# Second attention's projections in halves over sixteen units, weight splits in quarters, and GpSimd's adding transfers behind the norm pairs of the third attention

## The reference, cut to what matters

```python
x = x + tanh(g_xattn[1]) * _L1_xattn_ref(_layernorm(x), ctx, wq, wk, wv, wo, ln_w)   # second attention
x = x + tanh(g_ffn[1])   * _L1_ffn_ref(_layernorm(x), base_W, gate_W, lora_A, lora_B)
x = x + tanh(g_xattn[2]) * _L2_xattn_ref(_layernorm(x), ctx, Wq, bq, Wk, bk)         # third attention
x = x + tanh(g_ffn[2])   * _L2_ffn_ref(_layernorm(x), w1, w2, w3)

def _L1_xattn_ref(hidden_states, ctx, wq, wk, wv, wo, ln_w):
    x = rmsnorm(hidden_states, ln_w)
    q = (x @ wq.T)  in 32 heads of 16;  k, v = ctx @ wk.T, ctx @ wv.T  in 8 heads of 16, each for 4 query heads
    attn = softmax(q @ k.T / sqrt(16))                  # 256 tokens x 64 keys, per head and batch
    return concat(attn @ v) @ wo.T

def _L2_ffn_ref(x, w1, w2, w3):                         # w1, w2, w3 first rounded to 4-bit NF4 codes
    return (silu(x @ dq(w1).T) * (x @ dq(w2).T)) @ dq(w3).T
```

## Time and profile before

| | |
|---|---|
| median of 3 executions | 1507.81 us (1503.71 to 1510.55) |
| the profiled execution | 1506.91 us |
| its span, first to last instruction | 1505.2 us |
| TensorE busy | 1345.6 us, 89% of the span |
| VectorE busy | 1123.2 us, 75% |
| ScalarE busy | 677.1 us, 45% |
| GpSimd busy | 339.4 us, 23% |
| mean granted clock of TensorE | 0.952 of 2.4 GHz |

### The profile page before, as it was taken

One profiled execution on the slowest core, in us unless ns is written; L12 is line 12 of the kernel. 1 busy time (PEld: TensorE's weight loads), 2 busy tenths in 40 slices (PEclk: granted clock), 3 DMA queues, 4 the chain that ended last, 5 costly groups with the idle time before them and its releaser, 6 DMA issues.

```text
span 1505.2 us, 18648 instructions
## 1 busy us (share of the span) xinstructions
PE 1345.6 (89%) x6492; PEld 966.2 (64%) x6492; DVE 1123.2 (75%) x2045; ACT 677.1 (45%) x1405; POOL 339.4 (23%) x380
## 2 busy tenths in 40 slices
PE   8999999999998989977999998999999999999105
PEld 5665566566575648736888875777777777777102
DVE  4788898888888996976555576666666566568998
ACT  4778777877433443432222224443434444443104
POOL 1112122212164020233111021312222212213620
PEclk9999999999999999988999998999999999999557
DMA  5678888788810011323211210101101101000001
GB/s 218 170 179 184 226 225 197 173 221 213 224 43 1 1 57 34 79 64 79 71 42 42 96 71 1 71 28 43 71 29 43 69 13 61 1 1 1 0 0 56
DMA packets 37910, 127.74 MB, mean 85 GB/s; under 512 B 4944, under 2 KB 10960, under 8 KB 31680
## 3 DMA queue, kind: packets, MB, share of 16 engines
q1 hardware_dynamic: 26304, 83.38, 16.0%
q0 software_dynamic: 11520, 43.26, 15.1%
HBM read 72.63 MB, written 10.75 MB: 55 GB/s over the span
## 4 chain that ended last, share of the span: by engine, by line
PE 57%; DVE 23%; DVEq 6%; ACT 6%; DMA 4%; issue 2%; POOL 1%; POOLq 1%; SPq 0%
PE PS L150 12%; PE PS L152 11%; PE PS L151 11%; DVE AR L676 5%; PE PS L925 4%; PE PS L963 4%; DMA AR<-AR 3%; ACT s_sb L606 2%; DVE AR L2601 2%; PE PS L949 2%; DVE AR L2590 2%; DVE AR L2597 2%; DVEq L666 2%; DVE AR L682 1%; PE PS L535 1%
## 5 line engine op out<-in xcount | busy, mean ns | idle before, releaser
L438 POOL DMA_DIRECT2D AR<-AR x76 | 75.7, 1127 | 334.4 <-DMA AR<-AR 133.5
L151 PE MATMUL PS<-R16r 128*128 128x512 f32 (+1 forms) x328 | 122.1, 372 | 0.0
L535 PE MATMUL PS<-R,PT 128*128 128x512 f32 x256 | 116.1, 596 | 3.7 <-DVE X L716 3.7
L510 PE MATMUL PS<-R,HT 128*128 128x256 f32 x512 | 116.5, 381 | 3.2 <-ACT R L595 3.1
L152 PE MATMUL PS<-R16r 128*128 128x512 f32 (+1 forms) x312 | 119.1, 382 | 0.0
L510 PEld LDWEIGHTS PS<-R,HT 128*128 128x128 f32 x512 | 94.8, 190 | 16.2 <-ACT R L595 4.6
L1083 ACT COPY AR<-PS 128x512 f32<-128x512 f32 x64 | 37.5, 586 | 146.1 <-PE PS L152 145.7
L606 ACT ACTIVATE s_sb<-PS,sm 128x64 f32<-128x64 f32 x256 | 78.2, 338 | 53.4 <-DVE sm L701 52.8
L150 PE MATMUL PS<-HTr,R16r 128*128 128x512 f32 (+1 forms) x240 | 90.7, 378 | 4.6 <-DVE R16r L190 2.5
L150 PE MATMUL PS<-R16r,HTr 128*128 128x512 f32 (+1 forms) x224 | 90.2, 403 | 0.0
L152 PE MATMUL PS<-HTr,R16r 128*128 128x512 f32 (+1 forms) x240 | 87.7, 365 | 0.0
(11 more groups left out here) (313 smaller groups left out, 3495.0 us busy)
## 6 DMA issues: line engine op xcount, KB each, us to landing
AR<-AR POOLq DMA_DIRECT2D x76, 528.0 KB, 6.7
OR<-in_wo SPq DMA_DIRECT2D x12, 1024.0 KB, 12.4
dequantised<-AR SPq DMA_DIRECT2D x8, 1056.0 KB, 5.5
WR<-in_w0q SPq DMA_DIRECT2D x8, 1024.0 KB, 11.5
AR<-in_w3q SPq DMA_DIRECT2D x8, 1024.0 KB, 4.9
WR<-dequantised SPq DMA_DIRECT2D x22, 256.0 KB, 2.8
AR<-in_nf SPq DMA_DIRECT2D x4, 1056.0 KB, 9.4
nf_in<-in_nf SPq DMA_DIRECT2D x4, 1056.0 KB, 10.6
```

Source lines behind the costliest of these rows:

```text
L151: nc.tensor.matmul(out, ah, bl, start=False, stop=False)
L438: nc.gpsimd.dma_start(nf_below(g)[:, part], what[:, part], accum_op=ALU.add, max_dma_last_dim=4 * N_NF // 2).then_inc(added, 16)
L510: i = nc.tensor.matmul(bank(2 + u % 2)[:, tt * 256:(tt + 1) * 256], HT0[:, c, tok], m[:, :, c * B + b, :], start=c == 0, stop=c == C - 1)
L535: i = nc.tensor.matmul(bank(5 + tt), PT[:, at:at + P], vo[:, pr, b, :], start=pr == 0, stop=pr == 1)
```

## The change

In the second attention the eight output tiles and the queries of batches 2 and 3 are cut into halves (12 matmuls with 256 columns, or 6 with 512), and `projections(u)` deals them over all sixteen units: one half in twelve of the units, two halves in units 3, 6, 8 and 14. The adds on VectorE move with them. GpSimd's two weight splits become four quarters each, where a quarter also waits for a count of `probs`, that is, for a `norm` on VectorE to have ended. ScalarE's two copies for the feed-forward's weights move from units 8 and 9 to 7 and 8. At the third attention's end GpSimd's second adding transfer moves behind the norm pairs, a wait for all normed tiles of norm 4 stands in front of `pool_f2(pool, (1,))`, and two calls of `dve_stats` on VectorE move behind `norm_scaled` and `norm_low` calls.

```diff
@@ -1476,7 +1476,12 @@
             spread_keys(pool, 2)
             spread_keys(pool, 3)
             pool.wait_ge(A1["o_hi"], 1)
-            pool_low(Oh[:], Ol[:], OR[:]).then_inc(A1["o_split"], 1)
+            for c in range(C):
+                cols = slice(c * D, (c + 1) * D)
+                if c:
+                    pool.wait_ge(A1["probs"], c)
+                i = pool_low(Oh[:, cols], Ol[:, cols], OR[:, cols])
+            i.then_inc(A1["o_split"], 1)
 
         def u_kbd(hc, b):
             at = (hc * B + b) * HC1 * SK
@@ -1511,19 +1516,18 @@
             return (ORr[:, 0:HG * S], ORr[:, HG * S:2 * HG * S]) if b % 2 else (OTh, OTl)
 
         def pe_a1(pe):
-            def project_q(b, pr):
-                if b:
+            def project_q(b, pr, halves=(0, 1)):
+                if b and halves[0] == 0:
                     pe.wait_ge(A1["qT_ready"], 2 * b - 1 + pr)
-                if b >= 3 and pr == 1:
-                    pe.wait_ge(A1["acc"], 2 * b - 4)
-                for hh in range(2):
+                for hh in halves:
                     hc = 2 * pr + hh
                     for c in range(C):
                         w = slice(c * D + hc * P, c * D + (hc + 1) * P)
                         tok = slice(b * S, (b + 1) * S)
                         i = mm3(bank(1 - pr)[:, hh * S:(hh + 1) * S], Wh[:, w], Wl[:, w], HTh[:, c, tok],
                                 HTl[:, c, tok], c == 0, c == C - 1)
-                i.then_inc(A1["q_mm"], 1)
+                if halves[-1]:
+                    i.then_inc(A1["q_mm"], 1)
 
             def scores(u):
                 b, hc = divmod(u, C)
@@ -1557,21 +1561,53 @@
                                          PT[:, pr * S:(pr + 1) * S], start=True, stop=True)
                 i.then_inc(A1["pv_mm"], 1)
 
-            def project_o(b, tt):
-                if tt == 0:
-                    pe.wait_ge(A1["olo"], (b + 1) * C)
-                    if b == 0:
-                        pe.wait_ge(A1["o_split"], 1)
+            def project_o(b, tt, halves=(0, 1)):
+                if halves[0] == 0:
+                    if tt == 0:
+                        pe.wait_ge(A1["olo"], (b + 1) * C)
+                        if b == 0:
+                            pe.wait_ge(A1["o_split"], 1)
+                    else:
+                        pe.wait_ge(A1["qT_ready"], 2 * B)
+                    if b:
+                        pe.wait_ge(A1["acc"], 2 * b - 1 + tt)
+                hi, lo = out1(b)
+                for half in halves:
+                    for hc in (2 * half, 2 * half + 1):
+                        tok = slice(hc * S + tt * P, hc * S + tt * P + P)
+                        i = mm3(bank(0 if tt else 7), hi[:, tok], lo[:, tok], Oh[:, hc * D:(hc + 1) * D],
+                                Ol[:, hc * D:(hc + 1) * D], hc == 0, hc == C - 1)
+                if halves[-1]:
+                    i.then_inc(A1["wo_mm"], 1)
+
+            def projections(u):
+                if u < 2:
+                    project_q(2, 0, (u,))
+                elif u == 2:
+                    project_q(2, 1, (0,))
+                elif u == 3:
+                    project_q(2, 1, (1,))
+                    project_q(3, 0, (0,))
+                elif u == 4:
+                    project_q(3, 0, (1,))
+                elif u == 5:
+                    project_q(3, 1, (0,))
+                elif u == 6:
+                    project_q(3, 1, (1,))
+                    project_o(0, 0, (0,))
+                elif u == 7:
+                    project_o(0, 0, (1,))
+                elif u == 8:
+                    project_o(0, 1)
+                elif u < 13:
+                    project_o(1, (u - 9) // 2, ((u - 9) % 2,))
+                elif u == 13:
+                    project_o(2, 0, (0,))
+                elif u == 14:
+                    project_o(2, 0, (1,))
+                    project_o(2, 1, (0,))
                 else:
-                    pe.wait_ge(A1["qT_ready"], min(2 * b + 6, 2 * B))
-                if b:
-                    pe.wait_ge(A1["acc"], 2 * b - 1 + tt)
-                hi, lo = out1(b)
-                for hc in range(C):
-                    tok = slice(hc * S + tt * P, hc * S + tt * P + P)
-                    i = mm3(bank(0 if tt else 7), hi[:, tok], lo[:, tok], Oh[:, hc * D:(hc + 1) * D],
-                            Ol[:, hc * D:(hc + 1) * D], hc == 0, hc == C - 1)
-                i.then_inc(A1["wo_mm"], 1)
+                    project_o(2, 1, (1,))
             pe.wait_ge(A1["w_split"], 1)
             pe.wait_ge(lo_ready, T + 2)
             project_q(0, 0)
@@ -1592,10 +1628,7 @@
             for u in range(NU):
                 b, at = divmod(u, C)
                 turn_p(u)
-                if at < 2 and b:
-                    project_o(b - 1, at)
-                if at > 1 and b + 2 < B:
-                    project_q(b + 2, at - 2)
+                projections(u)
                 if u == NU - 1:
                     pe_norm_tile(pe, 3, 0)
                     pe_norm_tile(pe, 3, 1)
@@ -1668,8 +1701,8 @@
                 nc.scalar.copy(PT[:], bank(4, 2)).then_inc(A1["pt_ready"], 1)
                 if u + 2 < NU:
                     exps(u + 2)
-                if at > 1 and b + 2 < B:
-                    queries(b + 2, at - 2)
+                if u in (1, 3, 5, 7):
+                    queries(2 + u // 4, u // 2 % 2)
                 act.wait_ge(A1["pv_mm"], u + 1)
                 if u == C:
                     act.wait_ge(A1["o_split"], 1)
@@ -1677,11 +1710,11 @@
                 if u == NU - 2:
                     act_a2_keys(act, 0)
                     act_a2_keys(act, 1)
-                if u == 8:
+                if u == 7:
                     act.wait_ge(F1["w_in"], 16)
                     act.wait_ge(A1["q_mm"], 2 * B)
-                    nc.scalar.copy(Wh[:, 0:C * NWF // 2], WR[:, 0:C * NWF // 2])
-                if u == 9:
+                    nc.scalar.copy(Wh[:, 0:C * NWF // 2], WR[:, 0:C * NWF // 2]).then_inc(F1["w_hi"], 1)
+                if u == 8:
                     nc.scalar.copy(Wh[:, C * NWF // 2:C * NWF], WR[:, C * NWF // 2:C * NWF]).then_inc(F1["w_hi"], 1)
 
         def act_a2_keys(act, dc):
@@ -1724,14 +1757,24 @@
                 hi, lo = out1(b)
                 nc.vector.tensor_tensor(lo[:, cols], bank(6)[:, 0:S], hi[:, cols].bitcast(F32), ALU.subtract)\
                     .then_inc(A1["olo"], 1)
-                if 0 < hc < 3 and b:
-                    add(b - 1, hc - 1)
-                    if hc == 2:
-                        dve_stats(dve, b - 1)
+                if u == 8:
+                    add(0, 0)
+                elif u == 9:
+                    add(0, 1)
+                    dve_stats(dve, 0)
+                elif u == 11:
+                    add(1, 0)
+                elif u == 13:
+                    add(1, 1)
+                    dve_stats(dve, 1)
+                elif u == 15:
+                    add(2, 0)
             norm_low(dve, 3, 0)
             norm_scaled(dve, 3, 2)
+            add(2, 1)
             norm_low(dve, 3, 1)
             norm_scaled(dve, 3, 3)
+            dve_stats(dve, 2)
             add(B - 1, 0)
             add(B - 1, 1)
             dve_stats(dve, PAIRS - 1)
@@ -1756,17 +1799,22 @@
             sp.dma_start(OR[0:EH, 0:2 * D], lb_d).then_inc(F1["b_in"], 16)
 
         def pool_f1(pool):
-            pool.wait_ge(F1["w_hi"], 1)
-            pool_low(Wh[:, 0:C * NWF], Wl[:, 0:C * NWF], WR[:, 0:C * NWF]).then_inc(F1["split"], 1)
+            for c in range(C):
+                cols = slice(c * NWF, (c + 1) * NWF)
+                pool.wait_ge(A1["probs"], NU // 2 + c)
+                pool.wait_ge(F1["w_hi"], c // 2 + 1)
+                i = pool_low(Wh[:, cols], Wl[:, cols], WR[:, cols])
+            i.then_inc(F1["split"], 1)
             pool_norm(pool, 3)
             accumulate(pool, LATE, 1)
-            accumulate(pool, LATE, 2)
             pool_norm_pair(pool, 4, 0)
             pool_norm_pair(pool, 4, 1)
             pool_f2(pool, (0,))
             pool_norm_pair(pool, 4, 2)
             pool_norm_pair(pool, 4, 3)
+            accumulate(pool, LATE, 2)
             accumulate(pool, LATE, 3)
+            pool.wait_ge(hn_ready, T * 5)
             pool_f2(pool, (1,))
             pool_norm(pool, 5)
             accumulate(pool, LATE, 4)
@@ -2096,12 +2144,11 @@
             norm_scaled(dve, 5, 0)
             norm_scaled(dve, 5, 1)
             sums((6, 7))
+            norm_scaled(dve, 5, 2)
+            norm_low(dve, 5, 0)
+            norm_scaled(dve, 5, 3)
+            norm_low(dve, 5, 1)
             dve_stats(dve, 2)
-            norm_low(dve, 5, 0)
-            norm_low(dve, 5, 1)
-            norm_scaled(dve, 5, 2)
-            norm_scaled(dve, 5, 3)
-            dve_stats(dve, 3)
 
 
 
@@ -2316,6 +2363,7 @@
             norm_low(dve, 5, 3)
             norm_scaled(dve, 5, 4)
             norm_scaled(dve, 5, 5)
+            dve_stats(dve, 3)
```

## The result

The changed kernel takes 1496.91 us (median of 6 runs, 1495.79 to 1498.74) where the kernel before takes 1508.7 (median of 6 beside it, 1501.99 to 1510.78): a ratio of 0.9934, 95% interval 0.9917 to 0.995. The forecast was 1494.0, range 1488.5 to 1500.5. Its profiled execution has a span of 1494.0 us (1495.79 with what lies around it) for 1505.2 before.

What follows compares the result with a forecast made beforehand. VectorE and TensorE were taken to bound the second attention by turns, a chain through all engines the third attention's end. Gains 7.8 + 3.6 + 1.6 = 13.0 us off 1506.9 gave 1494, range 1488.5 to 1500.5.

Steps and rivals of the forecast that it cites:

- Second attention, 7.8 forecast: Units 0 to 15 and last outputs: halves hidden in TensorE's idle time gain 8.85 us, less 1.05 at the outputs.
- Unit 14, 7.35 forecast: Second attention: two halves make `weigh` late with the key wait behind it, so the unit takes 7.35 us, not 5.5.
- The quarters never meet a multiply: Second attention: each GpSimd quarter, some 1.7 us, ends before VectorE's next multiply; being late costs up to 1.7.
- rival 3: Second attention: TensorE's clock falls once in the loop or quarters meet a multiply; 3 to 4 us, 1497.5, chance 0.16.
- the idle 3.13: Second attention: TensorE's 3.13 us idle while GpSimd's whole split holds VectorE's multiply; rows at 1.2 GHz follow; expected to go.
- Third attention's end, 3.6 forecast: Scalings moved behind both `norm_scaled`: 3.6 us gained of the 6.0 or 4.4 the chain would give.
- The stall: Third attention, second half: GpSimd's scalings now hold VectorE's L360, which ends at 665.5 where it ended at 669.2.
- rival 2: Third attention's end: VectorE gets in between GpSimd's instructions; second part gives 6.0, total 1491.5, chance 0.16.
- rival 4: Third attention's end: second addition lands after 6.7 us, delaying third addition and scalings; 1497.5 to 1500, chance 0.12.
- rival 6: Behind the touched stages: something unseen gives the gain back; 1502 to 1507, chance 0.05.
- Statistics, 1.6 forecast: Before the third feed-forward: one statistics call moves behind the last low part, so TensorE's first product starts 1.6 us sooner.
- Rivals 3 and 5: rival 3 has its line; 5: the clock stays down in the second attention's loop, 3.2 us per unit, chance 0.05.

Runs made afterwards that it cites:

- e4: The changed kernel with both of GpSimd's weight splits whole again instead of in quarters: 1502.2 us, ratio 0.9961.
- e5: The kernel before with only GpSimd's two weight splits of the second attention cut into quarters: 1506.61 us, ratio 0.9992.
- e1: The kernel before with only the second attention's part of the change (halves, moved adds, quarters, earlier copies): 1502.52 us, ratio 0.9971.
- e6: The changed kernel with a GpSimd drain behind the first and second of the second weight tile's three scalings: 1497.24 us, ratio 0.9937.
- e7: The changed kernel with GpSimd's second weight tile's scalings waiting until VectorE is past the second half's L360: 1494.56 us, ratio 0.9909.
- e11: The kernel of e8 measured again, beside the changed kernel on the same chip: 1493.6 us, ratio 0.991.
- e2: The kernel before with only GpSimd's new order at the third attention's end: 1504.75 us, ratio 0.9979.
- e10: The changed kernel unaltered, measured and profiled a second time: 1497.34 us, ratio 0.9938.
- e3: The kernel before with only the two statistics calls moved later on VectorE: 1507.26 us, ratio 0.9996.
- e8: As e7, with the first weight tile's scalings also waiting for the first `norm_scaled` pair: 1493.98 us, ratio 0.9913.

## Why the prediction was right

**Second attention, 7.8 forecast, 7.0 and 6.7 measured** (loop and output step, 102.16 before, 95.13 and 95.46 after). A half is hidden and the unit is VectorE's: yes, 5.51. Unit 14, 7.35 forecast: 7.47. Unit 10, 7.85; units 11 to 13, 17.25 together for 17.15. Off by little everywhere: two halves cost 0.75 and not 0.6, in units 3 and 6, and the step to the last outputs 1.23, not 1.05. The quarters never meet a multiply, and what the whole split cost was seen rightly as L360's 2.35 us: e4 and e5 have 2.4. But the prediction, and its rival 3 with it, tied the rows at 1.2 GHz in the earlier trace rows to the idle 3.13. In e5 that idle time is gone (0.77), and the `scores` are at 1.2 GHz all the same (3.78, as in the kernel before). In the changed kernel, with half a piece ahead of `weigh`, they take 1.99 behind an idle 2.02; in e1, e6, e7 and e11 the clock falls there. What decides it stays open.

**Third attention's end, 3.6 forecast.** The chain did what was worked out, with the clock up: from the pair to L360 6.0 us less (15.63 to 9.61). The stall took the place foreseen: L360 of the second half 3.01 for 0.43, 2.6 back, 3.4 left. The Trainium skill ("SBUF — State Buffer", Who interferes with whom) has the loser of the shared port pair block for the other's instruction. That agrees with the rows of the kernel before shown with e6, where VectorE waits for one instruction of a run (L676 3.03 for 2.36); at the second weight tile's scalings it does not, for there VectorE waited for all three (5.13 for the pair before, L360 3.01, and 3.21 in e2). So rival 2's mechanism is real on this chip, and the trace that the prediction read had it at 640.65, beside the case against it at 653.6; for the scalings that counted it was wrong, and nothing in the prediction says why, so that this term came out right by the nearest row and not by an understood cause. Its 2.4 us were real: e7 gets 2.58 in that column by moving the scalings out of the way. The third addition waited for the second: its two halves were issued 5.5 and 8.5 us after the second's first issue (644.68 to 650.17 and 653.15), and the scalings began 9.0 after it, forecast 8.8. In this two errors cancel. The second addition's later half took 7.4 us to land, not 6.7 at most, which is rival 4's beginning; and the scalings followed the last issue by 0.57, where 1.33 behind the first of two had been put in.

What the forecast had not seen lies between the first feed-forward and that pair, in "end 1": either the first `norm_scaled` pair is held by GpSimd's first scalings (0.75, in the changed kernel's first profile), or TensorE's clock falls behind an idle time of 2 us (1.2 to 1.7), or both (e6, 19.79). The clock falls in nine of the ten profiles of a kernel with a changed second attention (e10 among them, not the first) and in none of the three with the old one (before, e2, e3), though the code and the idle time there are the same (2.06 in e1 and in e3): it may be a cost of the first part that comes 70 us later. That would be a piece of rival 6; no run here tells it from chance. Of the 3.5 us of the mechanism the columns "ff1", "end 1" and "end 2" keep 2.8 in the first profile and 2.0 in the second.

**Statistics, 1.6 forecast, 1.8 measured**, in both profiles of the changed kernel and in e3. Behind that product TensorE idles only ahead of the next one, 1.12 us as before; but its step from one to the other is 11.41 us for 10.98, at a granted clock of 0.78 for 0.81, so that up to 0.4 of the 1.8 may have gone there.

**Sum.** Touched stages: 7.0 + 2.8 + 1.8 = 11.6 in the first profile, 6.7 + 2.0 + 1.8 = 10.5 in the second, for 13.0; the medians differ by 11.8 and 10.3. The spans differ by 11.2 and 12.5, the rest being the start (+2.0 and +1.6), the third feed-forward (-0.4 and -0.3), "att 4" (-1.2 and +2.0) and what follows it (-0.7 and -1.2). The terms mis-sized are the first, by 0.8 to 1.1, and the second, which took the stage's clock as given, by 0.8 to 1.6. How near the total came is in part luck: start and "att 4" alone, which nothing touches, differ by 3 to 5 us from profile to profile. Rivals 3 and 5: the clock falls once in the loop in some executions (unit 10's step is 8.3 to 8.4 for 7.85 in e1, e6, e7 and e11, not in e8, the same kernel as e11), for 0.5 us and not 3 or 4, and it never stays down.

## What to carry to other kernels

Where VectorE is held by a run of GpSimd's instructions, put the run behind the next instruction of VectorE that reads two inputs from SBUF: here that was worth 2.6 us in its stage (e7), while cutting the run up with drains was worth nothing (e6), because the drain waited for a transfer. Ask at each new place which two-input instruction comes next, and look whether GpSimd has issued an adding transfer just ahead of a drain that something waits for. Work that fills a shared unit should be dealt out by each unit's slack: a half in every unit where VectorE is the bound, two where it has additions to make, one in the unit where a wait stands behind TensorE's work. And read an edit of 1 to 3 us in its own stage, between two milestones: here the span alone would have called e3 a loss.
